# Moving the router of an attention and mixture-of-experts layer within the hand-written order of one NeuronCore

## The chip, the cores and the metric

The kernel runs on one core of a Trainium2 chip. The metric is the device time of one execution in microseconds (us), the median of three runs. Everything is computed in float32, with matmuls split in high and low parts (`F32R`, three products for one) where TensorE would round.

## What is computed

`x` has 16 sequences of 256 tokens and 128 features. One layer is applied:

```python
x = x + attention(layernorm(x))      # 16 heads, 16 key dims, 64 value dims
x = x + moe(layernorm(x))            # 16 experts of width 64, and a shared one of width 128
# attention, per head
queries, keys, values = l2norm(queries), l2norm(keys), l2norm(values)
attn = square(relu(queries @ keys.T))
out = tanh_norm(attn @ values) * tanh(silu(gates))       # then out @ Wout
# the router of moe
scores = sigmoid(x @ gate_kernel) + gate_bias            # 16 experts in 4 groups of 4
# a group's sum: its best two scores; keep the 2 best groups, then the 4 best experts in them
weight = 2.5 * kept / (sum(kept) + 1e-20)
y = sum_e weight[e] * down_e(silu(gate_e(x)) * up_e(x)) + shared(x)
```

## The kernel before

All weights stay in SBUF. One sequence (256 tokens) passes through six stages, and the program is a software pipeline over steps `s` from -2 to 17: in step `s` the attention core (A) works on sequence `s`, the projections (P) on `s+1`, layer norm (L) on `s+2`, the end of attention (O) on `s-1`, and the MoE (F) on `s-2`. Steps 4 to 13 are a loop of two steps a turn; the others are written out. F is in steps 2 to 17.

A step has eight slots, one for each pair of heads. In slot `k` TensorE (PE) first does the filler jobs that the table `FILL` lists for it, then the scores of pair `k+1` (L459, read by ScalarE's relu, squared by GpSimd at L326), then the values of pair `k` (L488). The filler jobs, by name: `qk`, `v`, `g` projections; `ones` and `nT` sums of squares; `rT`, `rB` turning and spreading the head scales; `y` the output projection; `x2T` the turned MoE input; `gu` 0 to 8 the gate and up projections of two experts each; `lg` the router's logits (L421); `cT` (L403) and `cB` turning and spreading the expert weights `cs`; `y2` the down projections (L432).

The jobs use four PSUM banks in turn, in the order of the table. A job may start when the job four places ahead of it has been read out (`wait_for_bank`). So the place of a job in `FILL` also sets which job it waits for. A `gu` job's bank is free when VectorE (DVE) has multiplied it (L840, `gate_up`), after ScalarE's silu (L582). ScalarE reads the jobs in the order of the same table; for `lg` it takes a tanh (L577).

DVE has an order of its own, written as one block of code for each slot. The pieces that matter:

- `route_scores` (L781 to L789, five instructions), `route_groups` (L797 to L805, seven), `route_experts` (L811 to L824 and `split`, L773 to L775): the router, one chain in which each instruction waits for the one before. It ends with `cs`, for which job `cT` waits.
- `norms_start` (L642, L643) and three `newton` rounds (L648 to L650): the reciprocal roots for the head norms; `head_norms` (L752 to L754), then ScalarE's tanh of `nn`, then `head_scales`, for which job `rT` waits.
- `gate_up([c])`: one L840, which frees the bank of `gu` number `c`; `gated_heads(k)`: L888; `scale_heads`: four L848, one for each `rB`, after which `y` may run; `scale_hidden`: four L858, one for each `cB`.

In slot 3 DVE does `head_scales`, `value_scales`, `gate_up([6, 7])`, `gated_heads(3)`, `gate_up([8])` and then `route_scores`; in slot 4 `scale_heads`, `gated_heads(4)`, the statistics of layer norm, `route_groups` and `route_experts`.

## Time and profile before

| | |
|---|---|
| median of 3 runs | 885.55 us (884.7 to 889.24) |
| the profiled execution | 887.03 us, of which 885.3 us span from first to last instruction |
| PE busy | 718.8 us, 81% |
| DVE busy | 617.9 us, 70% |
| ScalarE (ACT) busy | 439.3 us, 50% |
| GpSimd (POOL) busy | 331.7 us, 37% |
| TensorE clock granted, mean | 0.919 of full speed |
| share of the chain that ended last | PE 56%, DVE 29%, ACT 3%, DMA 2% |

Times in the rows are microseconds from the start of the span. Neither PE nor DVE is busy all the time, and they take turns in the chain, so a stretch is judged by what waits in it. The loop's two steps take 102.4 us together. Step 11 is used as one example and step 12 as the other; they differ in the clock that was granted.

### The profile page before, as it was taken

To read this page: it belongs to the slowest core of one execution; us is meant where nothing else is said; L and a number is where in the kernel's file an instruction comes from. 1 tells how busy PE (TensorE), PEld (TensorE's weight loads), DVE (VectorE), ACT (ScalarE), POOL (GpSimd) and SP (SyncE) were. 2 spreads that over 40 slices of the span, in tenths; PEclk is the share of its full clock that TensorE was granted. 3 is DMA by queue.
4 is the path that set the end of the run, shared out by engine and by line. 5 is a ranking of instruction groups with operands and counts; after the bars stand their busy time and mean duration, and the time that the engine had idled before them with its cause. 6 is when DMAs were issued, how large, how long until landed. Compare 5 with 4: busy or idle time off the path is not lost.

```text
span 885.3 us, 17105 instructions
## 1 busy us (share of the span) xinstructions
PE 718.8 (81%) x5160; PEld 539.3 (61%) x5160; DVE 617.9 (70%) x1964; ACT 439.3 (50%) x986; POOL 331.7 (37%) x335
## 2 busy tenths in 40 slices
PE   2387778797987889798887979788797979889867
PEld 2253456575665666666665756666675756666766
DVE  4556667867576786768678676866868676776774
ACT  3366556363554636464464636455364635634311
POOL 2145453434343352434334333434434333444100
PEclk9688889997999989999899979999899998999998
DMA  6955919064280915528091642809063370900000
GB/s 175 143 96 61 134 15 138 7 109 47 64 93 13 131 13 101 55 71 84 13 132 11 113 41 73 83 13 141 0 117 38 84 70 10 140 7 2 7 1 13
DMA packets 68464, 58.87 MB, mean 66 GB/s; under 512 B 8368, under 2 KB 68144, under 8 KB 68400
## 3 DMA queue, kind: packets, MB, share of 16 engines
q1 hardware_dynamic: 68400, 58.16, 44.2%
q8 instruction: 22, 0.36, 0.2%
q14 instruction: 42, 0.34, 0.2%
HBM read 39.27 MB, written 18.87 MB: 66 GB/s over the span
## 4 chain that ended last, share of the span: by engine, by line
PE 56%; DVE 29%; issue 8%; ACT 3%; DMA 2%; POOL 1%; SPq 1%; DVEq 0%; ACTq 0%; POOLq 0%
PE ps_a L488 12%; PE ps_f L351 9%; PE ps_f L353 7%; PE ps_f L352 7%; PE ps_s L459 5%; PE ps_f L432 5%; DVE it L858 3%; PE ps_f L409 3%; DVE ln_t L648 3%; PE ps_f L392 2%; DVE ln_t L649 2%; PE ps_f L403 2%; DVE ln_y L650 2%; DVE it L840 2%; DVE big L848 2%
## 5 line engine op out<-in xcount | busy, mean ns | idle before, releaser
L326 POOL TENSOR_TENSOR p<-r 128x512 f32<-128x512 f32 x256 | 262.4, 1047 | 470.8 <-ACT r L590 443.7
L488 PE MATMUL ps_a<-p,v 128*64 128x256 f32 x1024 | 164.1, 438 | 5.1 <-POOL p L326 3.0
L590 ACT ACTIVATE r<-ps_s 128x512 f32<-128x512 f32 x256 | 140.1, 604 | 48.1 <-PE ps_s L459 43.1
L488 PEld LDWEIGHTS ps_a<-p,v 128*64 128x64 f32 x1024 | 70.1, 150 | 52.1 <-issue 15.8
L840 DVE TENSOR_TENSOR it<-ps_f,it 128x256 f32<-128x256 f32 x144 | 58.9, 419 | 40.1 <-ACT it L582 34.4
L432 PE MATMUL ps_f<-wdown,it 128*128 128x128 f32 x576 | 76.7, 292 | 12.0 <-DVE it L858 12.0
L582 ACT ACTIVATE it<-ps_f 128x256 f32<-128x256 f32 x144 | 55.8, 387 | 60.8 <-PE ps_f L353 60.6
L432 PEld LDWEIGHTS ps_f<-wdown,it 128*128 128x128 f32 x576 | 72.5, 205 | 18.3 <-issue 11.0
L459 PE MATMUL ps_s<-qkt 64*128 64x256 f32 x512 | 73.1, 362 | 10.2 <-DMA qkt<-qk_rows 9.2
L336 POOL TENSOR_TENSOR v<-v,vs 128x512 f32<-128x512 f32 x64 | 66.7, 1044 | 24.4 <-DVE vs L763 24.4
L888 DVE TENSOR_TENSOR big<-ps_a,wt 128x256 f32<-128x256 f32 x128 | 51.9, 416 | 34.1 <-ACT big L599 21.8
L569 ACT ACTIVATE rt<-ps_f 32x256 fp32r<-32x256 f32 x32 | 11.9, 373 | 127.2 <-PE ps_f L403 127.2
L459 PEld LDWEIGHTS ps_s<-qkt 64*128 64x128 f32 x512 | 43.9, 207 | 43.3 <-issue 23.0
L599 ACT ACTIVATE big<-ps_a 128x256 f32<-128x256 f32 x128 | 50.0, 391 | 32.5 <-PE ps_a L488 17.6
L557 ACT ACTIVATE wt<-ps_f 128x512 f32<-128x512 f32 x64 | 38.3, 599 | 51.1 <-PE ps_f L353 50.8
L729 DVE TENSOR_REDUCE norms_m<-sq 128x8 f32<-128x512 f32 x64 | 43.9, 686 | 28.2 <-ACT sq L551 28.1
L413 PEld LDWEIGHTS ps_f<-wout,big 128*128 128x128 f32 x512 | 58.4, 192 | 8.1 <-issue 5.4
L413 PE MATMUL ps_f<-wout,big 128*128 128x128 f32 x512 | 61.4, 278 | 2.1 <-DVE big L848 2.1
L351 PE MATMUL ps_f<-x2h,weg_hi 128*128 128x256 f32 x144 | 49.6, 345 | 15.1 <-DVE it L840 14.4
L848 DVE TENSOR_TENSOR big<-ps_f,big 128x512 f32<-128x512 f32 x64 | 41.1, 686 | 27.4 <-PE ps_f L409 27.4
L858 DVE TENSOR_TENSOR it<-ps_f,it 128x512 f32<-128x512 f32 x64 | 41.1, 686 | 26.1 <-PE ps_f L409 24.9
L409 PEld LDWEIGHTS ps_f<-rt,sel 128*128 128x128 f32 x256 | 42.4, 224 | 23.2 <-issue 18.6
(154 smaller groups left out, 1578.3 us busy)
## 6 DMA issues: line engine op xcount, KB each, us to landing
qk_rows<-qk_parts SPq DMA_DIRECT2D x16, 1024.0 KB, 4.4
qkt<-qk_rows SPq DMA_DIRECT2D x64, 256.0 KB, 10.0
qkt<-qk_rows SPq DMA_DIRECT2D x128, 128.0 KB, 9.4
x_in<-in_L_attn_tokens SPq DMA_DIRECT2D x16, 128.0 KB, 2.3
out<-o_sb SPq DMA_DIRECT2D x16, 128.0 KB, 1.9
big<-in_L_attn_Wqg SPq DMA_DIRECT2D x1, 640.0 KB, 4.3
big<-in_L_attn_Wkv SPq DMA_DIRECT2D x1, 640.0 KB, 6.8
big<-in_L_ffn_w_gate SPq DMA_DIRECT2D x1, 512.0 KB, 7.1
```

The source lines that it names most:

```text
L326: pool.tensor_tensor(p[h % 4][:], r[h % 2][:], r[h % 2][:], ALU.mult).then_inc(probs_done, 1)
L336: pool.tensor_tensor(view, view, broadcast(scale, [P, NP, DV], 2), ALU.mult)\
L351: pe.matmul(dst, stat[0], mov[0], start=True, stop=False)
L352: pe.matmul(dst, stat[0], mov[1], start=False, stop=False)
L409: last = pe.matmul(ps[:, c * N:(c + 1) * N], sel[:, 2 * j + c, :], rt[:], start=True, stop=True)
L413: last = pe.matmul(ps[:, 0:D], aw[pb][:, c, tok[j]], wout[:, c, :], start=(c == 0), stop=(c == NP - 1))
L432: last = pe.matmul(ps[:, 0:D], it[:, c, tok[j]], wdown[:, c, :], start=(c == 0), stop=(c == FC - 1))
L459: last = pe.matmul(ps_s[e][:, t * N:(t + 1) * N], qkt[q][rows, 1, k, t * P:(t + 1) * P], qkt[q][rows, 0, k, :], start=True, stop=True)
L488: last = pe.matmul(ps_a[k % 2][64 * e:64 * e + 64, 0:N], v[q][:, t, h * DV:(h + 1) * DV], p[h % 4][:, t * N:(t + 1) * N], start=(t == 0), ...
L590: act.activation(r[h % 2][:], ps_s[h % 2][:], ACT.Relu).then_inc(relu_done, 1)
L840: dve.tensor_tensor(it[:, c, :], bank[("gu", c)][:, N:2 * N], it[:, c, :], ALU.mult)\
L858: dve.tensor_tensor(part, bank[("cB", j)][:].rearrange("p (c n) -> p c n", n=N), part, ALU.mult).then_inc(read["cB"], 1)
```

## The change

`lg` moves from behind `gu` 2 in slot 2 to behind `gu` 0 in slot 1. The bank numbers of the jobs from there to `gu` 2 change with it. On DVE, `route_scores` moves from the end of slot 3 to slot 1, `route_groups` from slot 4 to slot 3 ahead of `gate_up([6, 7])`, and `route_experts` from slot 4 to slot 3 ahead of `gate_up([8])`. The order written for the last step alone is taken out.

```diff
     FILL = [
         [("P", "qk", 0), ("P", "v", 0), ("P", "qk", 1), ("P", "v", 1)],
-        [("F", "gu", 0), ("N", "ones", 0), ("P", "v", 2), ("F", "gu", 1), ("N", "nT", 0), ("P", "v", 3)],
-        [("F", "gu", 2), ("F", "lg", 0), ("F", "gu", 3), ("F", "gu", 4), ("F", "gu", 5)],
+        [("F", "gu", 0), ("F", "lg", 0), ("N", "ones", 0), ("P", "v", 2), ("F", "gu", 1), ("N", "nT", 0), ("P", "v", 3)],
+        [("F", "gu", 2), ("F", "gu", 3), ("F", "gu", 4), ("F", "gu", 5)],
...
-                if at == LAST_STEP:
-
-                    gate_up([0, 1, 2])
-                    route_scores(link_f, fb)
-                    route_groups(link_f)
-                    gate_up([3, 4, 5])
-                    route_experts(link_f, fb)
-                    link_f.end()
-                    gate_up([6, 7, 8])
-                    scale_hidden([0, 1, 2, 3])
-                    output_rows()
-                    return
-
...
                         if P_on:
                             sums(3, s + 1)
+                        if F:
+                            route_scores(link_f, fb)
                         if P_on or O:
                             norms_start(link_norms, P_on, O, s)
...
                         if F:
+                            route_groups(link_f)
                             gate_up([6, 7])
                         gated_heads(k)
                         if F:
+                            route_experts(link_f, fb)
+                            link_f.end()
+                        if F:
                             gate_up([8])
-                        if F and at != B:
-                            route_scores(link_f, fb)
...
-                        if F and at == B:
-                            route_scores(link_f, fb)
-                        if F:
-                            route_groups(link_f)
-                            route_experts(link_f, fb)
-                            link_f.end()
```

DVE's instructions in slot 1 of the loop's first step, as the difference of the two orders (L729 is the last sum of squares, of the fourth `v` job; L642 is the first seed of the head norms; L728, L632 and L745 are the sequencer's own):

```order
 L728 REGISTER_ALU
 L729 TENSOR_REDUCE norms_m<-sq 128x8
+L781 SCALAR_TENSOR_TENSOR sc<-th,bias 128x32
+L632 ISA
+L786 TENSOR_TENSOR pairs<-sc 128x8x3
+L787 TENSOR_TENSOR pairs<-sc 128x8x2
+L788 TENSOR_TENSOR pairs<-sc 128x8
+L632 REGISTER_ALU
+L789 TENSOR_REDUCE gsum<-pairs 128x8
+L632 REGISTER_ALU
 L745 REGISTER_ALU
 L642 TENSOR_SCALAR norms_y<-norms_m 128x64
```

The five of `route_scores` now stand between the last sum and the seeds.

On DVE in slot 3 of the same step, from the end of `value_scales` (L761, L763) on:

```order
 L761 RECIPROCAL rk<-ssqk 128x32
 L763 TENSOR_TENSOR vs<-norms_y,rk 128x32
+L797 TENSOR_TENSOR gt<-gsum 128x32
+L798 TENSOR_TENSOR eq<-gsum 128x32
+L632 REGISTER_ALU
+L799 TENSOR_TENSOR eq<-eq,lower 128x32
+L632 REGISTER_ALU
+L800 TENSOR_TENSOR gt<-gt,eq 128x32
+L632 REGISTER_ALU
+L801 TENSOR_REDUCE rank<-gt 128x8
+L632 REGISTER_ALU
+L805 SCALAR_TENSOR_TENSOR cand<-rank,sc 128x16 x2
```

The seven of `route_groups` (L805 twice) now stand ahead of the multiplication L840 that frees the bank of `gu` 6. Behind that come L840 of `gu` 7, L888, then `route_experts`, then the L840 of `gu` 8 and the four L848.

On PE in slot 1 of a step that is written out, behind `gu` 0, with the semaphores that a job waits for (`gu_read` is raised by DVE's L840, `v_read` by ScalarE, `qk_read` by DVE in slot 0):

```order
-L392 MATMUL ps_f<-big,ones 32x256 [waits qk_squared,a2_done,v_read]
+L421 MATMUL ps_f<-wroute,xn 128x16 [waits w_lo,v_read]
+L421 MATMUL ps_f<-wroute,xn 128x16
+L392 MATMUL ps_f<-big,ones 32x256 [waits qk_squared,a2_done,qk_read]
...
-L351 MATMUL ps_f<-x2h,weg_hi 128x256 [waits w_lo,v_read]
...
-L397 MATMUL ps_f<-pick,x_1 128x48 [waits ones_read,gu_read]
...
+L351 MATMUL ps_f<-x2h,weg_hi 128x256 [waits w_lo,gu_read]
...
+L397 MATMUL ps_f<-pick,x_1 128x48 [waits ones_read,lg_read]
```

`gu` 1 (the L351 here) waited for the second `v` job and now waits for DVE's multiplication of `gu` 0. By the same shift `gu` 5 in slot 2, which waited for `gu` 2, now waits for the fourth `v` job.

## Rows read from the trace of the kernel before

**Rows 1.** Waits: engine, line, waited for: us in total, times, longest.

```profile
PE ps_f L403 <- DVE cs L775: 38.1, 15, 3.0
PE ps_f L403 <- DVE it L840: 25.1, 15, 2.0
```

**Rows 2.** Stretches of steps 11 and 12: length, busy by engine, PEclk, DMA.

```profile
core 0: us, PE busy (x) PEld busy (x) DVE busy (x) ACT busy (x) POOL busy (x), PEclk, DMA share, GB/s
614.18:621.39 7.21, 7.21 (x46) 4.65 (x46) 4.79 (x15) 4.01 (x9) 3.04 (x3) 0.77 0.68 73
621.39:628.18 6.79, 3.84 (x34) 3.68 (x33) 6.15 (x30) 0.80 (x3) 3.04 (x3) 0.97 0.00 0
628.18:639.86 11.68, 10.15 (x59) 7.33 (x59) 9.07 (x27) 4.76 (x10) 6.08 (x6) 0.73 0.00 0
639.86:666.49 26.63, 23.80 (x186) 18.07 (x186) 17.40 (x50) 17.39 (x41) 8.25 (x8) 1.00 0.68 108
666.49:672.28 5.79, 5.79 (x46) 4.12 (x46) 4.80 (x15) 3.95 (x9) 3.04 (x3) 1.00 0.92 94
672.28:679.06 6.78, 3.84 (x35) 3.68 (x34) 6.14 (x30) 0.80 (x3) 3.04 (x3) 0.99 0.00 0
679.06:689.95 10.89, 8.85 (x58) 6.04 (x59) 8.58 (x27) 4.76 (x10) 6.08 (x6) 0.85 0.00 1
```

**Rows 3.** Timeline of PE in step 11: start, length, what [idle before, released by].

```profile
599.38 0.28 PE L351 MATMUL ps_f<-x2h,weg_hi 128*128 128x256 f32 x1
...
603.58 0.51 PE L421 MATMUL ps_f<-wroute,xn 128*128 128x16 f32 x4
...
606.54 0.39 PE L351 MATMUL ps_f<-x2h,weg_hi 128*128 128x256 f32 x1 [0.94 <-DVE it L840]
...
614.18 0.61 PE L403 MATMUL ps_f<-ident,rs 128*32 128x128 f32 x2 [1.74 <-DVE it L840]
...
628.18 0.58 PE L403 MATMUL ps_f<-ident,cs 128*32 128x128 f32 x2 [2.95 <-DVE cs L775]
```

**Rows 4.** Timeline of DVE in slots 1 to 3 of step 11.

```profile
599.48 0.42 DVE L840 TENSOR_TENSOR it<-ps_f,it 128x256 f32<-128x256 f32 x1 [1.94 <-ACT it L582]
...
603.26 0.90 DVE L642 TENSOR_SCALAR norms_y<-norms_m 128x64 int32<-128x64 int32 x1
...
609.78 0.97 DVE L753 TENSOR_TENSOR nn<-nn,rq 128x32 f32<-128x32 f32 x1
```

**Rows 5.** Timeline of POOL in slots 2 to 4 of step 11.

```profile
603.08 2.04 POOL L326 TENSOR_TENSOR p<-r 128x512 f32<-128x512 f32 x2 [3.64 <-ACT r L590]
608.66 2.04 POOL L326 TENSOR_TENSOR p<-r 128x512 f32<-128x512 f32 x2 [3.55 <-ACT r L590]
616.22 2.04 POOL L326 TENSOR_TENSOR p<-r 128x512 f32<-128x512 f32 x2 [5.51 <-ACT r L590]
618.22 1.05 POOL L336 TENSOR_TENSOR v<-v,vs 128x512 f32<-128x512 f32 x1
```

**Rows 6.** Timeline of DVE in slot 4 of step 11.

```profile
617.99 0.69 DVE L848 TENSOR_TENSOR big<-ps_f,big 128x512 f32<-128x512 f32 x1 [2.15 <-PE ps_f L409]
...
622.60 0.99 DVE L797 TENSOR_TENSOR gt<-gsum 128x32 f32<-128x32 f32 x1
623.51 1.08 DVE L798 TENSOR_TENSOR eq<-gsum 128x32 f32<-128x32 f32 x1
...
627.85 0.18 DVE L775 TENSOR_TENSOR cs<-comb,split_hi 128x32 f32<-128x32 f32 x1
```

**Rows 7.** Timeline of DVE in step 16, where POOL does nothing.

```profile
847.31 0.18 DVE L781 SCALAR_TENSOR_TENSOR sc<-th,bias 128x32 f32<-128x32 f32 x1
...
848.15 0.19 DVE L797 TENSOR_TENSOR gt<-gsum 128x32 f32<-128x32 f32 x1
...
849.46 0.18 DVE L814 MAX8 top<-cand 128x8 f32<-128x24 f32 x1
...
851.71 0.18 DVE L775 TENSOR_TENSOR cs<-comb,split_hi 128x32 f32<-128x32 f32 x1
```

**Rows 8.** Timeline of PE in step 16, job `cT`.

```profile
852.04 0.38 PE L403 MATMUL ps_f<-ident,cs 128*32 128x128 f32 x2 [0.69 <-DVE cs L775]
```

## The prediction

> **What bounds the kernel now.** I read three views in this order. The list of waits says for what PE stands still: 38.1 us in 15 waits for the expert weights `cs`, and 25.1 us in 15 waits of the same line for a multiplication L840, which is job `rT` [rows 1]. The timeline of PE puts them in the step: in step 11, `gu` 5 is held 0.94 us, `rT` 1.74 us, `cT` 2.95 us [rows 3]. The table of stretches gives what each part costs [rows 2]. Its stretches are, for step 11, `rT` to `y` (7.21 us), `y` to `cT` (6.79), `cT` to `x2T` (11.68), then `x2T` to the next `rT` (26.63), and for step 12 5.79, 6.78 and 10.89; the stretch that closes the pair is as long as the other of its kind. In `y` to `cT` PE is busy for only 3.84 of 6.79 us, and DVE for 6.15: there DVE is the bound, with the router in one piece, ending at 627.85 + 0.18 = 628.03 [rows 6]. After that idle time the granted clock of `cT` to `x2T` is 0.73 and 0.85, a mix of the full 2.4 GHz and of 1.2 GHz. The stretch `rT` to `y` has 0.77 in step 11 and 1.00 in step 12, behind nearly the same idle time of 1.74 us. From `x2T` to `rT` the clock is full, and PE is busy 23.80 of 26.63 us.
>
> A third thing is to be seen in DVE's rows. Small instructions that need 0.2 us alone take 1 us while POOL works: L642 is 0.90 us long at 603.26, when POOL's pair began at 603.08; L753 0.97 us within the pair of 608.66; L797 0.99 and L798 1.08 us [rows 4 to 6]. L797 alone takes 0.19 [rows 7]. The multiplications that read PSUM do not show this (L840 at 599.48 and L848 at 617.99 have the 0.42 and 0.69 us of all their kind). So an instruction of DVE on SBUF alone ends about when POOL's current instruction ends, and each POOL instruction catches one.
>
> **The change, part by part.** I follow one step of the steady part. There are 12 with the full wait at `cT`, steps 2 to 13.
>
> *Slot 1 on PE.* `lg` stands ahead of `ones`: 0.51 us with its drain [rows 3], I take 0.4. `gu` 1 now needs L840 of `gu` 0, which ran from 599.48 to 599.90, while `gu` 1 began at 599.38 [rows 3, 4]. ScalarE's silu for it comes behind `ones`, so both move 0.4 later and the gap of 0.5 stays as a wait, 0.6 with the restart. The fourth `v` job, its squares and DVE's last sum come 1.0 us later. Given back in slot 2: `lg`'s 0.4 us and the 0.94 of `gu` 5, whose bank now hangs on `v`. PE reaches the scores of slot 2 about 0.4 us earlier than before, and so does POOL's pair of 608.66.
>
> *Slot 1 on DVE.* The five of `route_scores` take 848.15 - 847.31 = 0.84 us alone [rows 7]. POOL's pair of 603.08 comes 1.0 later too, so it catches the first two of them in place of the two seeds, which cost the same. The first Newton round and `gate_up([2])` are 1.0 + 0.9 = 1.9 us late. `gu` 6, held by that multiplication now, hardly feels it.
>
> *Slot 2 on DVE.* The second Newton round would begin near 608.4, and POOL's pair now begins near 608.3. Two of its three instructions wait, to about 610.3. Before, that pair caught two of `head_norms`, behind `gate_up([4])`; now the same loss stands ahead of `gate_up([3])`, for which `gu` 7 waits some 1.6 us, and `g` 0 and `gu` 8 stay about 2.2 us late. `nn` and its tanh with them. If POOL's pair missed the round, this term would be 1.0 in place of 2.2; if it also caught a later one, 3.2.
>
> *Slot 3.* `route_groups` takes 849.46 - 848.15 = 1.31 us [rows 7] ahead of `gate_up([6])`, with POOL idle. Waiting behind it: both L840, L888, `rT`, then all scores and values of slots 3 and 4. `rT` is 2.2 + 1.3 = 3.5 us later. Bounds: 1.8 (the scores and the collision hidden but for half a us) and 4.5.
>
> *`rT` to `y`.* `route_experts` is 851.89 - 849.46 = 2.43 us alone [rows 7]. DVE had 2.15 us idle here before the first L848 [rows 6], which is its cover. But it stands ahead of `gate_up([8])`, for which the second `rB` waits, and POOL runs three instructions from 2.04 us to 5.09 us behind `rT` [rows 3, 5]. The L840 pair and L888 take 1 us from just before `rT`, so two thirds of `route_experts` are through when POOL begins; the last four instructions (L824 and `split`) meet POOL's three. If each of the three catches one, `cs` is ready 5 us behind `rT` and `gate_up([8])` is done at 5.3; if only two are caught, at 4.3. I take the first, since L642, with a single input, was caught like those with two [rows 4]. From the first L848 to `y` it was 621.39 - 617.99 = 3.4 us [rows 2, 6]. `y` starts 8.7 us behind `rT` (7.7 at the low end), +1.5 us in a step like 11 and +2.9 in one like 12.
>
> The Trainium skill, "SBUF — State Buffer", section "Who interferes with whom", says that DVE and GpSimd share one pair of ports, that an instruction with two SBUF inputs, or a copy, cast or tensor_scalar in a two-port mode, is blocked whole by a GpSimd instruction that reads SBUF, and that a reduction never is. The rows agree for L642, L753, L797 and L798; no row of this case shows a cast or a copy beside POOL. By the page all three POOL instructions catch one (8.7 us); were cast and copy free, it would be 7.7.
>
> *`y` to `cT`.* `cs` is ready before `y` starts, so `cT` follows the 3.84 us of `y` [rows 2]: 3.9 in place of 6.8, -2.9 us in each step. That is the whole of the wait of rows 1.
>
> *`cT` to `x2T`.* PE does not come out of an idle time here, so the clock should stay full. A mean of 0.73 over 11.68 us means 6.3 us at half clock, 0.85 over 10.89 means 3.3; at most 3.1 and 1.6 us are to be had. But the end of this stretch is DVE's chain of layer norm, which does not know the clock. I take half: -1.6 and -0.8.
>
> *Sum.* Like step 11: 3.5 + 1.5 - 2.9 - 1.6 = +0.5 us; like step 12: 3.5 + 2.9 - 2.9 - 0.8 = +2.7. Mean +1.6, times 12 = +19 us.
>
> *The end.* In step 16 there is no POOL, and the wait at `cT` is only 0.69 us [rows 8]; groups and experts, 3.7 us, stand ahead of `gate_up([8])` and `y`, against that 0.69 and some idle time: +2.5. Steps 14 and 15 lie between (their waits at `cT` are near 1 us): +2 each. In step 17 DVE has the same instructions in another order and is the bound in both: 0. Together +6.5.
>
> The sum is made against the profiled execution, 887.03 us (885.3 and 1.7 around it), 1.5 us above the median: 887.0 + 25.7 = 912.7, or 911 against the median of 885.55. I take **910 us**.
>
> **The rivals.**
>
> *The wait at `cT` goes and nothing takes its place (faster).* For it: 2.9 us of idle PE and the half clock behind it are real, and DVE has 1.94 us idle before its first L840 and 2.15 in slot 4 [rows 4, 6]. Against it: the first idle time lies ahead of the sums, where `route_scores` can't use it, and `gu` 5 and `rT` already wait for DVE. It holds if `rT` slips only by the groups and 0.5 (+1.8), `y` by 0.5 more, and the clock in `rT` to `y` does not fall: 1.8 + 0.5 - 2.9 - 1.2 = -1.8 a step, -22 us and +5 at the end: 868 us. It decides as long as `y` slips by less than 4.1 us (2.9 + 1.2). Chance 0.20.
>
> *Loss and gain cancel within 4.4 us (half a per cent, about what a measurement of this kernel can tell).* The low ends of both slots: 2.5 + 1.2 - 2.9 - 1.2 = -0.4 a step, +1: 886 us. Chance 0.07.
>
> *It gets worse than forecast.* The longer idle time before `rT` (3 us where 1.74 was) brings half clock into `y` as well, and the seeds of layer norm behind `y` meet POOL's pair: 1 us each, +3.4 a step, 885.6 + 41 + 6.5 = 933 us. Chance 0.13. The Trainium skill, "TensorE: Matmul & The Clock Gate", describes a gate that cuts the clock by half when PE has been idle; that step 12 kept its clock behind 1.66 us and step 11 did not behind 1.74 is what this trace shows of it, and behind 2.95 us both lost it.
>
> **How the numbers follow.** The forecast (`rT` 2.5 to 4.5 us later) has 0.60, with a range of its own of 898 to 922. Faster 0.20, same 0.07, slower 0.60 + 0.13 = 0.73. For 8 in 10 I leave out the lower half of the faster case and most of the worst case: 877 to 924.
>
> **What would show it.** In the profile after: no wait of L403 for `cs`; L403 for `rT` held 3 us or more by L840; a new wait of `gu` 1 near 0.5 us and of `gu` 7 near 1.6 for L840; none at `gu` 5; L648 or L649 of the norms near 1 us long in the second round and L642 near 0.2; L824 and `split` long; clock of `rT` to `y` below 1 in every step and of `cT` to `x2T` near 1; `x2T` to `rT` near 30.1 us; `y` to `cT` 3.9. The prediction is wrong if POOL's pair misses the second Newton round, so that `rT` slips by less than 2.5 us, or if `route_experts` ends before POOL begins.

## The result and the profile after

The changed kernel takes 947.82 us (median of 4 runs, 947.16 to 949.77); the kernel before took 887.39 us beside it (884.7 to 890.39, 4 runs). The ratio is 1.068, with a 95% interval of 1.064 to 1.073: 60 us slower, where 24 were forecast. The profiled span grew from 885.3 to 945.6 us, the mean granted clock of TensorE fell from 0.919 to 0.892 of full speed. Of the executions behind the times below, one of `w_idle` (985.84 us, at a granted clock of 0.646 where its others have 0.93) is left out as a slow one.

The waits of PE (engine, line, waited for: us in total, times, longest):

```profile
PE ps_f L403 <- DVE it L840: 44.3, 15, 3.6
PE ps_f L351 <- DVE it L840: 38.2, 53, 2.0
PE ps_f L432 <- DVE it L858: 34.2, 16, 2.4
...
PE ps_f L418 <- DVE xn L667: 5.3, 2, 4.7
...
PE ps_f L403 <- DVE cs L775: 3.2, 1, 3.2
```

Of the kernel before, beside [rows 1]:

```profile
PE ps_f L418 <- DVE xn L667: 21.0, 14, 4.6
PE ps_f L351 <- DVE it L840: 14.4, 22, 0.9
PE ps_f L432 <- DVE it L858: 12.0, 10, 2.4
```

The 38.1 us for `cs` of [rows 1] are gone but for one wait in the last step. In their place stand 44.3 us of `rT` (before 25.1 [rows 1]), 38.2 us of the `gu` and `g` jobs (before 14.4), and 34.2 us of `y2` (before 12.0). The wait of `x2T` (L418) for layer norm, 21.0 us in 14 steps before, is left in 2. The stretches of step 11, `x2T` to `rT`, `rT` to `y`, `y` to `cT`, `cT` to `x2T`, with the columns of [rows 2]:

```profile
616.65:647.49 30.84, 24.52 (x188) 18.52 (x187) 18.53 (x59) 17.42 (x41) 8.16 (x8) 0.99 0.73 105
647.49:655.98 8.49, 7.73 (x47) 5.19 (x47) 8.12 (x27) 4.01 (x9) 3.04 (x3) 0.80 0.21 21
655.98:659.65 3.67, 3.67 (x34) 3.66 (x33) 1.81 (x7) 0.80 (x3) 3.04 (x3) 1.00 0.00 0
659.65:670.59 10.94, 8.59 (x61) 6.54 (x59) 9.76 (x28) 4.70 (x10) 6.04 (x6) 0.92 0.00 0
```

Against [rows 2] the third stretch is 3.1 us shorter; the first is 4.2 us longer, the second is 1.3 us longer than in step 11 before and 2.7 longer than in step 12, and the last, where a gain was forecast, is as long as the shorter of the two before (10.89). The timeline of PE in step 11 (start, length, what, [idle before, released by]) shows where the first stretch grew:

```profile
629.61 0.39 PE L351 MATMUL ps_f<-x2h,weg_hi 128*128 128x256 f32 x1 [0.42 <-DVE it L840]
...
640.37 0.39 PE L351 MATMUL ps_f<-x2h,weg_hi 128*128 128x256 f32 x1 [1.48 <-DVE it L840]
...
641.90 0.39 PE L351 MATMUL ps_f<-xh,wg_hi 128*128 128x256 f32 x1 [0.56 <-DVE it L840]
...
647.49 0.39 PE L403 MATMUL ps_f<-ident,rs 128*32 128x128 f32 x2 [3.64 <-DVE it L840]
...
648.24 1.97 PE L488 MATMUL ps_a<-p,v 128*64 128x256 f32 x8
```

`gu` 1, `gu` 7, `g` 0 and `rT` wait, and behind the 3.64 us the products with `v` take 1.97 us, at a granted clock of 0.51; at full clock the same eight take 1.08 (at 660.40). On POOL and DVE of the same stretch (two views, POOL's first):

```profile
633.42 2.04 POOL L326 TENSOR_TENSOR p<-r 128x512 f32<-128x512 f32 x2 [4.70 <-ACT r L590]
637.38 2.04 POOL L326 TENSOR_TENSOR p<-r 128x512 f32<-128x512 f32 x2 [1.92 <-ACT r L590]
649.02 2.04 POOL L326 TENSOR_TENSOR p<-r 128x512 f32<-128x512 f32 x2 [9.59 <-ACT r L590]
651.01 1.04 POOL L336 TENSOR_TENSOR v<-v,vs 128x512 f32<-128x512 f32 x1
```

```profile
633.49 1.02 DVE L781 SCALAR_TENSOR_TENSOR sc<-th,bias 128x32 f32<-128x32 f32 x1
634.55 0.96 DVE L786 TENSOR_TENSOR pairs<-sc 128x24 f32<-128x24 f32 x1
...
637.77 0.73 DVE L648 TENSOR_TENSOR norms_t<-norms_m,norms_y 128x64 f32<-128x64 f32 x1
638.54 0.96 DVE L649 SCALAR_TENSOR_TENSOR norms_t<-norms_t,norms_y 128x64 f32<-128x64 f32 x1
...
647.00 0.76 DVE L840 TENSOR_TENSOR it<-ps_f,it 128x256 f32<-128x256 f32 x2 [0.47 <-DVE cand L805]
...
649.33 0.75 DVE L822 TENSOR_SCALAR den<-den 128x2 f32<-128x2 f32 x1
650.12 0.17 DVE L823 RECIPROCAL den<-den 128x2 f32<-128x2 f32 x1
650.32 0.79 DVE L824 SCALAR_TENSOR_TENSOR comb<-chosen,den 128x32 f32<-128x32 f32 x1
651.13 0.96 DVE L773 CAST split_hi<-comb 128x32 fp32r<-128x32 f32 x1
```

POOL's pair of 633.42 catches two of `route_scores`, the pair of 637.38 two of the second Newton round, and the three instructions from 649.02 on catch L822, L824 and the cast. `route_groups` lies free of POOL, but 0.47 us of idle time follow it. I call an instruction held when POOL's work makes it longer like this.

In the first stretch the held ones are four (L781, L786, L648, L649), 3.67 us long where the same four take 0.82 alone: 2.85 us lost. Before, that stretch had four held ones too, L642 and L753 of [rows 4] and these:

```profile
604.20 0.96 DVE L643 TENSOR_SCALAR norms_y<-norms_y 128x64 int32<-128x64 int32 x1
...
609.14 0.61 DVE L752 TENSOR_TENSOR nn<-norms_m,norms_y 128x32 f32<-128x32 f32 x1
```

They are 3.44 us long, 0.77 alone: 2.67 us lost. So what POOL holds in the first stretch has moved to other instructions and has hardly grown.

For all kernels below I compare the same stretches, each number the mean over steps 4 to 13 of the distance between the starts of two of PE's jobs, and for the end the lengths of steps 14, 15, 16 (`x2T` to `x2T`) and from the last `x2T` to the last `cT`. All times are us.

| kernel | x2T-rT | rT-y | y-cT | cT-x2T | step | 14 | 15 | 16 | to cT |
|---|---|---|---|---|---|---|---|---|---|
| before | 26.80 | 6.65 | 6.79 | 11.28 | 51.52 | 48.70 | 39.26 | 30.19 | 11.97 |
| changed | 31.30 | 8.79 | 3.67 | 11.12 | 54.88 | 54.08 | 46.56 | 35.98 | 14.01 |
| a_fill | 27.68 | 6.67 | 6.80 | 11.07 | 52.21 | 49.79 | 39.91 | 31.64 | 12.90 |
| a_scores | 29.45 | 7.16 | 6.79 | 10.82 | 54.22 | 51.62 | 40.86 | 30.75 | 12.93 |
| a_groups | 30.76 | 7.37 | 4.31 | 10.74 | 53.18 | 53.00 | 42.53 | 34.68 | 13.37 |
| a_last | 26.65 | 6.66 | 6.79 | 11.19 | 51.30 | 48.71 | 39.26 | 30.18 | 15.31 |
| b_experts_behind | 31.10 | 8.53 | 3.68 | 10.85 | 54.16 | 53.81 | 44.01 | 35.54 | 14.25 |
| b_behind | 29.45 | 10.31 | 4.20 | 10.30 | 54.26 | 53.12 | 43.73 | 35.84 | 15.68 |
| w_idle | 26.92 | 7.15 | 4.31 | 10.69 | 49.06 | 48.34 | 38.52 | 32.94 | 12.11 |
| w_groups | 27.04 | 9.02 | 4.32 | 10.84 | 51.22 | 50.69 | 43.04 | 33.21 | 12.09 |
| ww_step16 | 26.94 | 7.05 | 4.30 | 10.75 | 49.05 | 48.42 | 38.60 | 31.91 | 12.62 |
| ww_more | 25.99 | 10.11 | 4.26 | 10.35 | 50.72 | 51.30 | 38.52 | 31.91 | 12.83 |
| mm_before | 25.88 | 7.22 | 5.55 | 9.13 | 47.78 | 46.12 | 36.24 | 30.80 | 12.63 |
| mm_after | 27.70 | 7.54 | 3.67 | 8.87 | 47.78 | 49.19 | 39.08 | 35.90 | 13.94 |
| e_from14 | 31.26 | 8.99 | 3.67 | 11.11 | 55.03 | 50.82 | 40.87 | 30.95 | 13.89 |
| e_from16 | 31.30 | 8.97 | 3.68 | 11.07 | 55.02 | 53.78 | 43.57 | 31.44 | 12.89 |

Steps 2 to 13 together grew by 37.8 us (618.1 to 655.9), steps 14 to the last `cT` by 54.08 + 46.56 + 35.98 + 14.01 - 48.70 - 39.26 - 30.19 - 11.97 = 20.5 us. The other 2.0 us of the span's growth lie ahead of step 2 and behind the last `cT`.

The second table is what DVE loses to holds in the same ten steps: for each of its instructions the length above the shortest of the same kind in any of these traces, where that is over 0.2 us, summed. It is us a step, with the number of instructions held.

| kernel | x2T-rT | rT-y | y-cT | cT-x2T |
|---|---|---|---|---|
| before | 2.6 (4.0) | 0 (0) | 2.3 (3.0) | 2.4 (3.5) |
| changed | 2.9 (4.0) | 2.1 (3.1) | 0.6 (0.9) | 3.0 (4.0) |
| a_fill | 2.3 (3.0) | 0 (0) | 2.3 (3.0) | 2.3 (3.3) |
| a_scores | 2.9 (4.0) | 0 (0) | 2.3 (3.0) | 2.3 (3.1) |
| w_idle | 2.6 (4.0) | 0.5 (0.8) | 1.1 (2.0) | 2.9 (4.0) |
| w_groups | 2.6 (4.0) | 2.4 (3.2) | 1.0 (1.8) | 3.0 (4.0) |
| mm_before | 0.7 (2.0) | 0 (0) | 0.9 (1.0) | 0.6 (1.0) |
| mm_after | 0 (0) | 0.8 (1.0) | 0 (0.2) | 1.6 (2.0) |

From before to changed the holds grow by 1.2 us a step, 14 us in steps 2 to 13, where the time grows by 37.8. They match the growth of `rT` to `y` (2.1 of 2.1 us), and not that of `x2T` to `rT` (0.2 of 4.5).

### The profile page after: what moved, and what is told of

It is laid out like the page before. It is cut to its first block, busy times and chain, and to the rows that moved or that the text cites. A ratio compares the mean times of both kernels' runs of the same rounds, so it can differ in the third digit from the quotient of the medians.

```text
span 945.6 us, 17123 instructions
## 1 busy us (share of the span) xinstructions
PE 751.0 (79%) x5160; PEld 571.0 (60%) x5160; DVE 640.1 (68%) x1964; ACT 440.0 (47%) x986; POOL 331.1 (35%) x335
## 4 chain that ended last, share of the span: by engine, by line
PE 48%; DVE 35%; issue 9%; ACT 4%; DMA 2%; POOL 1%; DVEq 1%; SPq 1%; ACTq 0%; POOLq 0%
PE ps_f L432 9%; PE ps_a L488 7%; PE ps_f L413 7%; PE ps_f L351 6%; PE ps_f L353 4%; PE ps_f L352 4%; DVE it L840 4%; DVE it L858 3%; PE ps_s L459 3%; PE ps_f L409 3%; DVE norms_t L649 2%; PE ps_f L392 2%; DVE ln_t L649 2%; DVE ln_y L650 2%; DVE ln_t L648 2%
## 5 line engine op out<-in xcount | busy, mean ns | idle before, releaser
L432 PE MATMUL ps_f<-wdown,it 128*128 128x128 f32 x576 | 91.1, 327 | 34.2 <-DVE it L858 34.2
L432 PEld LDWEIGHTS ps_f<-wdown,it 128*128 128x128 f32 x576 | 87.0, 239 | 40.8 <-issue 26.7
L488 PEld LDWEIGHTS ps_a<-p,v 128*64 128x64 f32 x1024 | 70.6, 147 | 53.8 <-issue 11.4
L840 DVE TENSOR_TENSOR it<-ps_f,it 128x256 f32<-128x256 f32 x144 | 59.4, 422 | 50.1 <-ACT it L582 41.3
L888 DVE TENSOR_TENSOR big<-ps_a,wt 128x256 f32<-128x256 f32 x128 | 52.1, 419 | 38.7 <-ACT big L599 24.9
L459 PE MATMUL ps_s<-qkt 64*128 64x256 f32 x512 | 69.6, 346 | 10.3 <-DMA qkt<-qk_rows 9.3
L351 PE MATMUL ps_f<-x2h,weg_hi 128*128 128x256 f32 x144 | 50.5, 351 | 32.4 <-DVE it L840 32.1
L729 DVE TENSOR_REDUCE norms_m<-sq 128x8 f32<-128x512 f32 x64 | 43.9, 686 | 37.8 <-ACT sq L551 37.8
L409 PE MATMUL ps_f<-rt,sel 128*128 128x256 f32 x256 | 55.3, 334 | 16.8 <-DVE it L840 13.4
L413 PEld LDWEIGHTS ps_f<-wout,big 128*128 128x128 f32 x512 | 61.8, 201 | 7.6 <-issue 6.1
L413 PE MATMUL ps_f<-wout,big 128*128 128x128 f32 x512 | 64.8, 287 | 1.2 <-DVE big L848 1.2
L459 PEld LDWEIGHTS ps_s<-qkt 64*128 64x128 f32 x512 | 41.2, 195 | 40.1 <-issue 19.1
L351 PEld LDWEIGHTS ps_f<-x2h,weg_hi 128*128 128x128 f32 x144 | 28.5, 198 | 60.5 <-DVE it L840 49.2
```

What stands on the lines that cost most here:

```text
L351: pe.matmul(dst, stat[0], mov[0], start=True, stop=False)
L409: last = pe.matmul(ps[:, c * N:(c + 1) * N], sel[:, 2 * j + c, :], rt[:], start=True, stop=True)
L413: last = pe.matmul(ps[:, 0:D], aw[pb][:, c, tok[j]], wout[:, c, :], start=(c == 0), stop=(c == NP - 1))
L432: last = pe.matmul(ps[:, 0:D], it[:, c, tok[j]], wdown[:, c, :], start=(c == 0), stop=(c == FC - 1))
L459: last = pe.matmul(ps_s[e][:, t * N:(t + 1) * N], qkt[q][rows, 1, k, t * P:(t + 1) * P], qkt[q][rows, 0, k, :], start=True, stop=True)
L488: last = pe.matmul(ps_a[k % 2][64 * e:64 * e + 64, 0:N], v[q][:, t, h * DV:(h + 1) * DV], p[h % 4][:, t * N:(t + 1) * N], start=(t == 0), ...
```

## The experiments

My theory: the time goes to DVE's small instructions on SBUF that are laid in front of, or pushed into, POOL's instructions. The rival: the pieces cost their own length wherever PE waits behind them, and the half clock that follows. A second rival, for `lg`, is the shift of banks alone. The second table above already says that both the theory and the first rival are needed: the theory for `rT` to `y`, the rival for `x2T` to `rT`.

### The change, put in piece by piece

**a_fill** is the kernel before with the new `FILL` alone.

```diff
-        [("F", "gu", 0), ("N", "ones", 0), ("P", "v", 2), ("F", "gu", 1), ("N", "nT", 0), ("P", "v", 3)],
-        [("F", "gu", 2), ("F", "lg", 0), ("F", "gu", 3), ("F", "gu", 4), ("F", "gu", 5)],
+        [("F", "gu", 0), ("F", "lg", 0), ("N", "ones", 0), ("P", "v", 2), ("F", "gu", 1), ("N", "nT", 0), ("P", "v", 3)],
+        [("F", "gu", 2), ("F", "gu", 3), ("F", "gu", 4), ("F", "gu", 5)],
```

> Only the FILL table of the change: the logits job stands in slot 1, VectorE's order is that of before. Theory 1 (the cost is what VectorE does ahead of the instructions that TensorE waits for, and what GpSimd's instructions catch of it): gu 1 waits 0.4 to 0.6 us for VectorE, gu 5 no longer waits 0.94 us, and the rest stays: within 0.3 us a step, 883 to 893 us. Rival 2 (the shift of the bank numbers is what costs, since gu 1 now hangs on VectorE): +1 us a step or more, above 900 us.

Measured: 901.71 us, 1.014 of before (1.010 to 1.018), outside the theory's range and in the rival's (above 900). In step 12, whose `x2T` of the step before is at 648.33, POOL's pair of 668.89 catches the third Newton round with one instruction, and the seeds stand later (the timeline of DVE):

```profile
665.12 0.91 DVE L642 TENSOR_SCALAR norms_y<-norms_m 128x64 int32<-128x64 int32 x1
...
670.01 1.00 DVE L648 TENSOR_TENSOR norms_t<-norms_m,norms_y 128x64 f32<-128x64 f32 x1
```

So moving `lg` costs 14 us by itself, and `rT` comes 0.9 us later. POOL's catch in the Newton round is not the reason, since the pair no longer catches the head norms: the stretch has three held instructions in place of four. The delay is there before: the seeds start 665.12 - 648.33 = 16.79 us behind `x2T`, before 15.73 (655.59 - 639.86), and from the seeds to `rT` it takes 10.86 us where it took 10.90. `lg` itself and the 0.42 us that `gu` 1 now waits for DVE stand ahead of the fourth `v` job, whose sum the seeds need, and what slot 2 gives back to PE doesn't bring DVE's chain forward. How much of it is the shift of banks and how much `lg`'s own length was not run apart.

**a_scores** adds the move of `route_scores` into slot 1.

```diff
                             sums(3, s + 1)
+                        if F:
+                            route_scores(link_f, fb)
...
-                        if F and at != B:
-                            route_scores(link_f, fb)
...
-                        if F and at == B:
-                            route_scores(link_f, fb)
```

> The FILL table and route_scores in slot 1; groups and experts stay in slot 4 as before. Theory 1: the first Newton round comes 1.9 us later, GpSimd's pair catches the second round, job rT slips 2 to 2.5 us, and nothing is given back at job cT, since groups and experts still stand there: +2.3 us in 12 to 14 steps, 912 to 922 us, with the wait at cT as long as before. Rival 2: no more than the table alone costs. Rival 3 (the clock is the cost, not the order): granted clock from rT to y falls in every step, and the time by the clock alone, +0.7 us a step, 895 us.

Measured: 928.45 us, 1.047 (1.042 to 1.052), above the theory's 912 to 922. 27 us for five instructions that are 0.84 us long. `rT` comes another 1.8 us later: 1.0 is their length with the 0.19 us idle behind them, 0.6 that POOL holds four instructions again in place of three. And since the rest of the router still stands behind `scale_heads`, the 6.79 us from `y` to `cT` stay. This piece brings nothing there alone.

**a_groups** adds `route_groups` ahead of `gate_up([6, 7])`.

```diff
                         if F:
+                            route_groups(link_f)
                             gate_up([6, 7])
...
-                            route_groups(link_f)
                             route_experts(link_f, fb)
```

> As the run before, and route_groups in slot 3 ahead of gate_up([6, 7]); route_experts stays in slot 4. Theory 1: rT slips by another 1.3 to 1.8 us (to 4 to 4.6 us in all), but at cT the groups and what GpSimd caught of them are gone (3.0 us), so the wait at cT falls from 2.95 to below 1 us: about equal to the run before, 910 to 922 us; the rest of the way to 948 is then route_experts ahead of gate_up([8]) and the last steps. If the groups were the costly piece, it is above 930.

Measured: 920.91 us, 1.037 (1.034 to 1.041), as expected, 7.5 us less than a_scores. It is the only piece of the change that pays: `rT` comes 1.3 us later, `y` to `cT` is 2.5 us shorter. What is left of the change, `route_experts` ahead of `gate_up([8])` and the last step, then costs 27 us; of the wait it wins only another 0.64 us a step (4.31 to 3.67) and pays 1.4 from `rT` to `y` (7.37 to 8.79).

**a_last** is the kernel before without the last step's own order (those twelve lines of the change's diff).

> Only the order of the last step is taken out; the FILL table and the rest as before. The last step then runs scores behind gate_up([8]), scale_heads absent, and groups and experts in slot 4 in one piece: the expert weights come 2 to 4 us later than with the order of its own, all of it at the end of the program: +3 us, 890 us. A cost above 6 us would make it a main part of the 60 us.

Measured: 890.66 us, 1.003 (1.001 to 1.006). From the last `x2T` to the last `cT` it takes 3.3 us more (11.97 to 15.31). That the order of the last step is free, as forecast, is wrong, but it is a small part of the 60 us.

### The experts, put behind what PE waits for

**b_experts_behind** and **b_behind** are the changed kernel with `gate_up([8])` ahead of `route_experts`, and with both the groups and the experts behind `gate_up([8])`.

```diff
                         if F:
+                            gate_up([8])
                             route_experts(link_f, fb)
                             link_f.end()
-                        if F:
-                            gate_up([8])
```

> The changed kernel with gate_up([8]) ahead of route_experts in place of behind it. Theory 1 (VectorE's time ahead of the four L848 is what counts, whoever frees the bank): the second rB no longer waits, but the L848 start when route_experts is through: 0 to -0.5 us a step, 940 to 948 us. If the bank of gu 8 were the cause, TensorE would win 1 us a step or more with the clock behind it: 930 us.

> The changed kernel with route_groups and route_experts both behind gate_up([8]) in slot 3. Theory 1: rT comes 1.8 us earlier (1.3 of the seven instructions and 0.5 of the wait behind them), but both now stand ahead of the L848 and meet GpSimd's three instructions, so rT to y grows by 1 to 1.5 us: 938 to 945 us.

Measured: 939.13 us, 1.057 (1.053 to 1.062), a little below what I expected, and 941.42 us, 1.059 (1.055 to 1.063), as expected. The order at `gate_up([8])` is worth 9 us of the 60. With the groups behind it too, `rT` comes 1.9 us earlier, but `rT` to `y` takes 1.5 us more: groups and experts then both stand between `rT` and the first L848. Moving pieces back by a few places doesn't mend the change.

### The same pieces in DVE's idle time, and 1 us later

**w_idle** is the kernel before with `route_scores` ahead of `head_scales` in slot 3, where DVE waits for ScalarE's tanh, and `route_groups` behind `gate_up([8])`; the experts stay in slot 4. **w_groups** has the same groups in the same place, but the scores stay just ahead of them.

```diff
                     if k == 3:
+                        if F:
+                            route_scores(link_f, fb)
                         if O:
                             head_scales(link_o, b)
...
                             gate_up([8])
-                        if F and at != B:
-                            route_scores(link_f, fb)
+                            route_groups(link_f)
```

> From the kernel before (logits in slot 2, own last step kept): route_scores at the head of slot 3, into the 0.75 us in which VectorE waits for ScalarE's tanh of nn; route_groups behind gate_up([8]), into the 2.15 us of idle time ahead of the first L848 and ahead of GpSimd's pair; route_experts stays in slot 4. Theory 1 (a piece is free where VectorE idles, GpSimd is still, and no L840 stands behind it): job rT within 0.3 us of before, the expert weights about 2.3 us earlier, the wait at cT below 1 us in place of 2.95: -2.4 us a step and up to 1 us of clock, 845 to 862 us. Rival 2 (any part of the router ahead of slot 4 delays rT or y by its own length, as in the changed kernel): no gain, 885 us or more.

> From the kernel before, only route_groups moves, from slot 4 to the place behind route_scores at the end of slot 3, where it begins about when GpSimd's pair begins. Theory 1: the pair catches two of its instructions there as it did in slot 4, so that the first L848 starts 0.7 to 1 us late, and 3.0 us in slot 4 are gone: -2 us a step at cT, 860 to 875 us. Without GpSimd's part it would be as fast as the run before. Rival 2: 885 us or more.

Measured: w_idle 859.6 us, 0.967 (0.962 to 0.972), faster than both kernels and in the theory's range; w_groups 891.51 us, 1.004 (1.001 to 1.007), far above the 860 to 875 that I expected and in the rival's range. The two differ by 32 us, 2.2 us a step. Both have the seven instructions of the groups in this place; w_groups has the five of the scores, 0.84 us long, just ahead of them. The timeline of DVE in step 11 of w_idle:

```profile
593.51 0.18 DVE L797 TENSOR_TENSOR gt<-gsum 128x32 f32<-128x32 f32 x1
...
594.50 0.84 DVE L805 SCALAR_TENSOR_TENSOR cand<-rank,sc 128x16 f32<-128x16 f32 x2
```

and in w_groups, where `rT` is at 610.63 in place of 592.65, and POOL's pair at 612.16 in place of 594.19:

```profile
612.33 0.93 DVE L797 TENSOR_TENSOR gt<-gsum 128x32 f32<-128x32 f32 x1
...
613.38 0.92 DVE L799 TENSOR_TENSOR eq<-eq,lower 128x32 f32<-128x32 f32 x1
614.34 0.97 DVE L800 TENSOR_TENSOR gt<-gt,eq 128x32 f32<-128x32 f32 x1
```

Measured from `rT`, POOL starts at the same moment (1.54 and 1.53 us behind). The groups start 0.86 us behind `rT` in the one and 1.70 us in the other. In the one POOL catches only the last of the seven (the L805 pair, 0.84 us), and they end 1.8 us after they began; in the other it catches three, and they take 3.5 us. So the groups end 2.50 us later behind `rT` in w_groups (5.19 against 2.69): 0.84 is the length of the scores, 1.66 is the place against POOL.

**ww_step16** is w_idle with step 16 in the order of before. **ww_more** moves `gate_up([6, 7])` ahead of `value_scales` besides, since PE waits 1.8 us for it ahead of `rT`.

```diff
                             link_o.end()
+                        if F:
+                            gate_up([6, 7])
                         if P_on:
                             value_scales(link_p, s + 1, rq2[pq])
                             link_p.end()
-                        if F:
-                            gate_up([6, 7])
```

> The kernel with scores ahead of the head scales of slot 3 and groups behind the last gate_up (860 us, 0.967 of before), with step 16 alone put back to the order before. Step 16 has no waiting for cT to win, and its stretch from x2T to rT and to cT was 2.75 us longer there than before. Theory 1: -2.5 us, 857 to 858.5 us. Rival: the order of step 16 does not matter, since the time lost there came with a clock at half for another reason: 860.

> ww_step16 with gate_up([6, 7]) moved ahead of the scales of the values and of the scores in slot 3. PE waits 1.7 us for those two multiplications ahead of rT. Theory 1: rT starts about 0.9 us earlier, the idle time ahead of it falls under 1 us, and the clock of rT to y is full in every step: -0.8 to -1.5 us a step, 838 to 850 us. Rival: the scores move 0.4 us later and meet POOL's instructions behind rT, or the products that wait for the scales of the values come later: 857 to 865.

Measured: ww_step16 857.6 us, 0.965 (0.961 to 0.969), the fastest kernel here that leaves no work out. It is 2.0 us below w_idle, but the two intervals overlap, so that a difference between them is not shown; in the table step 16 is 1.0 us shorter and the last stretch 0.5 longer. ww_more 884.54 us, 0.997 (0.994 to 1.000): far above the theory's 838 to 850 and above the rival's 857 to 865 as well. What the rival said would happen did, at a higher price. `rT` is 0.95 us earlier and its idle time falls from 1.82 to 0.90 us, but now the groups start 1.84 us behind it, with POOL's pair at 1.54 (DVE's timeline, step 11, `rT` at 604.60):

```profile
606.44 0.79 DVE L797 TENSOR_TENSOR gt<-gsum 128x32 f32<-128x32 f32 x1
...
607.36 0.92 DVE L799 TENSOR_TENSOR eq<-eq,lower 128x32 f32<-128x32 f32 x1
608.31 0.97 DVE L800 TENSOR_TENSOR gt<-gt,eq 128x32 f32<-128x32 f32 x1
```

Then `scale_heads` is late, and PE waits for it:

```profile
610.57 0.58 PE L351 MATMUL ps_f<-xh,wg_hi 128*128 128x256 f32 x1 [2.53 <-DVE big L848]
```

An earlier `rT` brought POOL forward too. The change took 0.9 us off the wait ahead of `rT` and made `rT` to `y` 3.1 us longer, of it 2.53 us this wait.

### GpSimd's reads taken away

**mm_before** and **mm_after** are the two kernels without POOL's square: one column is squared and the other 511 are filled with 0.5, so that these scores are not squared (lines below it move by one).

```diff
-                            pool.tensor_tensor(p[h % 4][:], r[h % 2][:], r[h % 2][:], ALU.mult).then_inc(probs_done, 1)
+                            pool.tensor_tensor(p[h % 4][:, 0:1], r[h % 2][:, 0:1], r[h % 2][:, 0:1], ALU.mult)
+                            pool.memset(p[h % 4][:, 1:512], 0.5).then_inc(probs_done, 1)
```

> The kernel before, with one alteration to the work: POOL's square of the scores' half (one 512-column instruction of about 1 us per job) is replaced by a one-column square and a fill of the other 511 columns with 0.5, so these scores are not squared; POOL's product with v stays. Theory 1 (DVE's small instructions are held by POOL's instructions that read SBUF): of each POOL pair only the product still holds a DVE instruction, so one of L797 and L798 falls from 1.0 to 0.2 us, y to cT falls from 6.8 us to 5.9 or less, and the kernel takes 860 to 880 us. Theory 2 (the long instructions have another cause, for instance reading what has only just been written): L797 and L798 stay near 1 us and the time stays within 5 us of the kernel before.

> The changed kernel with the same alteration (the square of the scores left out but for one column, the rest filled with 0.5). Theory 1 (most of the change's +60 us is that its pieces of routing are put before POOL's instructions, or push others before them): the distance to mm_before shrinks to +25 to +40 us, and L786, L649 and L824 are mostly short. Theory 2 (the change costs what the pieces cost by themselves, ahead of the multiplications that PE waits for, and the half clock behind that): the distance stays at +50 to +60 us.

Measured: mm_before 825.64 us, 0.929 of before (0.925 to 0.933), and mm_after 841.38 us, 0.948 (0.945 to 0.952). Both are below what I expected of them. The distance between the two is 15.7 us in place of 60, less than the 25 to 40 of the theory, and a step of the steady part takes 47.78 us in both: `rT` 1.8 us later and `y` 0.3 more, against 1.9 and 0.3 given back behind `y`. Steps 2 to 13 differ by 0.6 us, where they differed by 37.8. So the loss of the steady part needs POOL's squares, and what is left is in the end of the program.

That does not mean that the moved pieces are held more: by the table of holds they are not in `x2T` to `rT`. There the squares take away the idle time in which the pieces could hide. In step 11 DVE stands idle ahead of L768, for ScalarE's tanh (L769 here; mm_before, then mm_after):

```profile
567.76 0.19 DVE L769 TENSOR_TENSOR nn<-nn,bound 128x32 f32<-128x32 f32 x1 [1.96 <-ACT nn L606]
```

```profile
568.18 0.19 DVE L769 TENSOR_TENSOR nn<-nn,bound 128x32 f32<-128x32 f32 x1 [0.90 <-ACT nn L606]
```

Against `x2T` L769 is only 0.2 us later in mm_after (24.07 against 23.85), though the third Newton round is 1.3 us later: the lengths of `lg` and of the scores go into the 1.96 us. With the squares that idle time is 0.75 us before, and L768 is 2.5 us later in the changed kernel (27.07 against 24.61). The 1.8 us that are left in mm_after are those of the groups. From `rT` to `y` the holds fall from 2.1 to 0.8 us, and with them the growth from 2.1 to 0.3. DVE and POOL in step 11 of mm_after, where the experts meet POOL (two views):

```profile
573.79 0.36 DVE L823 TENSOR_SCALAR den<-den 128x2 f32<-128x2 f32 x1
...
574.38 0.19 DVE L825 SCALAR_TENSOR_TENSOR comb<-chosen,den 128x32 f32<-128x32 f32 x1
...
574.82 0.95 DVE L775 COPY cs<-split_hi 128x32 f32<-128x32 f32 x1
```

```profile
573.60 0.52 POOL L327 MEMSET p<- 128x511 f32 x1
...
574.21 0.53 POOL L327 MEMSET p<- 128x511 f32 x1
574.70 1.04 POOL L337 TENSOR_TENSOR v<-v,vs 128x512 f32<-128x512 f32 x1
```

L825 (the L824 of the changed kernel) starts inside a fill and takes 0.19 us in place of 0.79; the copy starts inside the product with `v` and takes 0.95. L823 starts inside a fill too and lasts as long as the fill does, 0.36 us where it needs 0.17. The test has a flaw that it can't shed: POOL's fill takes 0.52 us where the square took 1.0, so its results come earlier as well, and part of the 62 us between before and mm_before, and of what shrinks between the two kernels, may be that. PE's own waits for POOL are small in both real kernels (3.0 us in 7).

### The end of the program

**e_from14** and **e_from16** are the changed kernel with DVE's order of before from step 14, or from step 16, on.

```diff
+                OLD = at is not None and at >= 14
...
-                        if F:
+                        if F and not OLD:
                             route_scores(link_f, fb)
...
+                        if F and OLD and at != B:
+                            route_scores(link_f, fb)
```

(and so for the groups, the experts and the last step; 16 in place of 14 in the other).

> The changed kernel with VectorE's order of before in steps 14 to 17 (the last step's own order too); PE keeps lg in slot 1. Theory 1 (the pieces of routing cost in each of these steps, where little or no wait at cT is there to be won): of the +20.5 us of the end only what the move of lg by itself costs there stays (4 us in its own run), so 16 us less than the changed kernel, 929 to 934 us. Rival (the price forecast, +6.5, was right for the order, and the rest is carried over from the steps before): 4 to 7 us less, 941 to 944 us.

> The changed kernel with VectorE's order of before in steps 16 and 17 alone. Theory 1 (these two steps hold 5.8 + 2.0 us of the loss, of which lg's move made 2.3 by itself): 5 to 6 us less than the changed kernel, 941 to 943 us. Rival (the loss hangs on how step 15 ends): within 2 us of the changed kernel.

Measured: 932.42 us, 1.052 (1.048 to 1.057), and 939.67 us, 1.061 (1.058 to 1.064). Against the changed kernel's 947.82 that is 15.4 and 8.2 us less; by the ratios, 14 and 6.5. The stages of e_from14 give 14.1 us back in steps 14 to 17. So two thirds of the 20.5 us are made by DVE's order in these very steps. Of the 6.4 us that stay, a_fill has 4.1 by the move of `lg` alone; 2.3 are open. e_from16 gives back 5.7 us in steps 16 and 17; another 3.3 of its gain stand in steps 14 and 15, whose order it doesn't touch. There the clock differed: `y` to `cT` of step 15 takes 3.65 us at a granted clock of 1.00, in the changed kernel 4.77 at 0.76. So two profiled executions can differ by 3 us in one step of the same order. What the loss is made of can be read in step 16 of the changed kernel, which has no POOL:

```profile
899.97 1.65 PE L409 MATMUL ps_f<-rt,sel 128*128 128x256 f32 x6 [1.25 <-DVE it L840]
902.84 6.12 PE L413 MATMUL ps_f<-wout,big 128*128 128x128 f32 x32 [1.22 <-DVE big L848]
```

The experts ahead of `gate_up([8])` hold `rB` for 1.25 us, the L848 behind them hold `y` for 1.22, and `y` runs at a granted clock of 0.60: 6.12 us where it is 3.84 at full clock [rows 2].

## Why the prediction was wrong

The direction and the kind of trade were right: a wait at `cT` sold for longer ones ahead of it. The size was wrong by 36 us, in three terms: `x2T` to `rT` and the end were priced too low, and the gain from `cT` to `x2T` did not come, since the forecast followed the wrong engine there.

**`x2T` to `rT`, forecast +3.5, measured +4.5 a step.** The parts of it that were named are there: `gu` 1 waits 0.42 us (forecast 0.5), `gu` 7 1.48 (1.6), `gu` 5 no more, and the second Newton round is hit by POOL at two instructions. In step 11 that makes the end of `value_scales` 2.46 us later against `x2T`, near the forecast 2.2 (L763 at 645.17 - 616.65 = 28.52, before 26.06). The 2.46 are 1.1 for `lg` and `gu` 1's wait in slot 1 and 1.0 for the scores with 0.19 us of idle time behind them; the rest is small. The term that was sized too low is the groups, costed at 1.31 us from step 16. Here L840 comes 1.83 us behind L763, with 0.47 us of idle time ahead of it, where before it came 0.11 behind: +1.7. The remaining 0.3 of the mean is spread over steps that I did not take apart.

**`rT` to `y`, forecast to 8.7 us, measured 8.79**, and **`y` to `cT`, forecast -2.9, measured -3.1.** Both sizes held, and so did the reason: three POOL instructions catch three of the experts' chain, the cast among them. Two details were off and did no harm: POOL begins 1.53 us behind `rT` and not 2.04, when 1.0 us and not two thirds of the chain is through, and it catches L822, L824 and the cast and not only the last four. The Trainium skill, "SBUF — State Buffer", section "Who interferes with whom", names casts and copies in a two-port mode among what GpSimd can block; the rows now agree, with the cast of 0.96 us (changed kernel) and the copy of 0.95 (mm_after).

**`cT` to `x2T`, forecast -1.2, measured -0.2 a step.** The step that failed is the sentence that "the end of this stretch is DVE's chain of layer norm". It was so before: in step 11 `x2T` waited 1.53 us for it behind the end of `y2`. And the chain did come sooner, by about what was forecast: it ends 10.13 us behind `cT` in the changed kernel (669.78 - 659.65), before 11.53 in step 11 and 10.75 in step 12. But now `x2T` waits for PE's own `y2`: its waits for layer norm fell from 21.0 to 5.3 us, and those of `y2` for L858 rose from 12.0 to 34.2. `y2` starts no sooner than before, 7.97 us behind `cT` against 7.87 and 7.57, though the first L858 came 1.7 us sooner (2.40 us in place of 4.07 in step 11). Before, POOL's first three instructions fell mostly into the 2.1 us in which DVE waited for `cB`, 2 us of idle time followed, and the other three held three instructions of the second and third rounds. Now the six come back to back, from 662.10 to 668.14, and hold four (DVE's timeline, step 11 after):

```profile
663.25 0.90 DVE L648 TENSOR_TENSOR ln_t<-ln_m,ln_y 128x4 f32<-128x4 f32 x1
664.19 0.97 DVE L649 SCALAR_TENSOR_TENSOR ln_t<-ln_t,ln_y 128x4 f32<-128x4 f32 x1
665.19 0.96 DVE L650 SCALAR_TENSOR_TENSOR ln_y<-ln_t,ln_y 128x4 f32<-128x4 f32 x1
...
667.39 0.76 DVE L648 TENSOR_TENSOR ln_t<-ln_m,ln_y 128x4 f32<-128x4 f32 x1
```

The second pair of L858 stands behind the first round, `y2` waits 2.35 us for it, and then runs in part at half clock: 3.16 us in place of 2.27 before. What that clock costs can be read in w_idle, where `y2` also starts 7.97 us behind `cT` in each of the ten steps. The stretch `cT` to `x2T` in its steps 11 and 10:

```profile
604.26:614.53 10.27, 7.86 (x58) 5.68 (x59) 9.40 (x27) 4.70 (x10) 6.04 (x6) 1.00 0.00 0
554.46:565.73 11.27, 8.91 (x58) 6.93 (x59) 10.21 (x31) 4.70 (x10) 6.04 (x6) 0.89 0.00 1
```

Five of its ten steps take 10.27 us; there the forecast of about 1 us less than before (11.28) holds. The others take 10.8 to 11.4, as the changed kernel's do (10.7 to 11.6). With POOL's squares gone (mm_after) the stretch takes 8.87 us.

**The end, forecast +6.5, measured +20.5.** I priced step 16 from its wait of 0.69 us [rows 8] and set step 17 at 0. Measured: +5.4, +7.3, +5.8 and +2.0 us in steps 14, 15, 16 and the last. In steps 14 and 15 the forecast of +2 left out that they pay nearly the full price (`rT` 3.9 and 3.4 us later, `y` 2.9 and 3.9) with little at `cT` to win (1.2 and 0). In step 16 it left out the slower clock in `y`, 1.5 of the 5.8 us. e_from14 shows that 14.1 of the 20.5 us are this order in these steps.

Of the sum: 12 steps x 1.6 forecast against 37.8 measured is 18.6 us of the miss, about half of it from `rT` and half from `cT` to `x2T`; the end is 14; 2 us lie ahead of step 2 and behind the last `cT`.

**The rivals.** The faster case fell with its condition, since `rT` slipped by 4.5 and not 1.8 us. The worse case, 933 us, was nearest and still too low: half clock came, though not in `y` of the steady steps (1.00) but in `y2`. (Its parts, 1.6 and twice 1 us, make +3.6 a step and not +3.4; it would be 935.) Neither of the two signs that were to refute the forecast came: POOL's pair did not miss the second Newton round, and `route_experts` did not end before POOL began.

**What is shown and what is not.** Shown by runs: that the steady loss needs POOL's squares, by their reads and their length together (mm_before, mm_after); that the groups, begun 0.84 us later behind the scores, lose 1.66 us more to POOL (w_idle, w_groups); that two thirds of the end's loss are made in place (e_from14); and what half clock in `y2` costs with DVE at the same times (w_idle). Read from the traces, without a run that takes it alone: that from `x2T` to `rT` the pieces cost their own lengths and not more holds, because DVE has less than 1 us of idle time ahead of L768 to hide them. Not separated: how much of the other stretches' loss is the DVE delay and how much the half clock that PE falls to behind it.

## What to carry to other kernels

Before a small vector instruction is moved, ask two things of its new place. Does its engine have idle time behind it, before somebody waits? If not, it costs its whole length, as `lg` and the scores did here. And where does it stand against GpSimd? Here the same seven instructions took 1.8 or 3.5 us by where they stood against three GpSimd instructions. Remember that the GpSimd work moves too, since it hangs on the engine that is to be sped up: in ww_more `rT` came 1 us earlier and `y` 2 us later. And a late chain is best shortened by its first, independent pieces, put into waits on its own engine (w_idle, -3.3%), not by bringing its last pieces ahead of work that others wait for. When one engine's part of a stretch gets shorter, look for the engine that ends it next.

## What the hardware showed

- One GpSimd instruction that reads SBUF held one DVE instruction, back to back where both engines ran on: three in a row of 0.90 to 0.97 us, and behind an L858 pair a fourth of 0.76, that need 0.16. Tensor_scalar, cast, copy and everything with two SBUF inputs were held; RECIPROCAL (0.17 us at 650.12), reductions (L821, 0.19), and in w_groups MAX8 and MATCH_REPLACE8 (0.17 to 0.18) ran at their own length beside it. A GpSimd fill did not hold a two-input instruction (0.19 us), but it held a tensor_scalar to its end (L823 of mm_after, 0.36 us for 0.17). The Trainium skill, "SBUF — State Buffer", section "Who interferes with whom", states this of two-input instructions, that GpSimd blocks them only when it reads; the trace agrees.
- Behind `route_groups` DVE stood idle for 0.47 us in the loop's second step (steps 5, 7, 9, 11; 0.49 in 13), for 0.12 in its first (4, 6, 8, 10, 12), and for 0.03 to 0.04 in the steps written out (2, 3, 14 to 16), with the same instructions on both sides. So it is not the dependency by itself; what makes it is not shown. The seven instructions before it had gaps of 0.04 at most.
- Idle times of PE within 0.1 us of one another went with different clocks (full and half behind 1.66 and 1.74 us before), and even the same idle time did: 1.71 us ahead of `rT` in both steps 2 and 3, with 5.79 and 7.18 us from `rT` to `y`. So a stretch flips between two lengths, 5.8 and 7.2 us here. In mm_before, where this stretch takes 7.2 us each time, ten steps agree within 0.05 us.
